# Wo block: the transpose of the rows normalised for the feed-forward, and the two copies behind it, one row tile later

## The reference

```python
# x is (1, 2048, 1024); LN(v) = (v - mean) / sqrt(var + 1e-5) over the last axis
q, k, v = LN(x) @ Wq, LN(x) @ Wk, LN(x) @ Wv           # 16 heads of 64, rotary on q and k
attn = softmax(causal(q k^T) / 8) v                     # per head, then the heads side by side
x = x + LN(attn @ Wo)
gate, up = LN(x) @ Wg^T, LN(x) @ Wu^T                   # Wg, Wu, Wd: 4-bit codes and block scales
x = x + LN((silu(gate) * up) @ Wd^T)
```

## Time and profile before

| | |
|---|---|
| time, median of 3 runs | 3079.66 us (3079.39 to 3079.66) |
| time of the profiled execution | 3079.91 us |
| span of the profiled execution | 3078.1 us |
| mean granted clock of TensorE | 0.960 of full speed |
| PE, PEld, DVE, ACT, POOL busy | 89%, 48%, 68%, 59%, 20% of the span |
| the Wo block in the span | its first transpose starts at 1311.3 us, its last copy ends at about 1558.0 us |

### The profile page before, as it was taken

The page is one execution under the profiler, slowest core; times in us unless marked ns, Lnnn a source line. Parts: engine busy times, 40 slices in busy tenths (PEclk is TensorE's granted clock), DMA queues, the critical chain, the costliest instruction groups (busy, mean ns, idle before and its releaser), DMA issues. The chain is left out here.

```text
span 3078.1 us, 55127 instructions
## 1 busy us (share of the span) xinstructions
PE 2738.7 (89%) x19792; PEld 1476.4 (48%) x19792; DVE 2106.7 (68%) x3522; ACT 1830.1 (59%) x2483; POOL 601.1 (20%) x399
## 2 busy tenths in 40 slices
PE   4998999789999999588808999999999999999996
PEld 2443444267777777444403444444444444444442
DVE  6544555577777777345567877877777777777867
ACT  2113434268888988712267677766767667676642
POOL 0000000067778878500120000000000000000002
PEclk9998999789999999899959999999999999999998
DMA  4312222322222221112221111111111111111124
GB/s 164 119 51 89 82 75 68 89 77 77 77 76 62 73 75 49 59 62 75 74 64 55 49 50 48 48 55 46 52 49 49 50 49 48 55 50 45 53 69 164
DMA packets 84361, 209.43 MB, mean 68 GB/s; under 512 B 13840, under 2 KB 14224, under 8 KB 83856
## 3 DMA queue, kind: packets, MB, share of 16 engines
q1 hardware_dynamic: 84112, 206.17, 21.5%
HBM read 172.49 MB, written 33.62 MB: 67 GB/s over the span
## 5 line engine op out<-in xcount | busy, mean ns | idle before, releaser
L1334 PE MATMUL gp<-region,wgu 128*128 128x512 f16 x4224 | 930.3, 383 | 90.0 <-DVE wgu L1492 90.0
L1371 ACT ACTIVATE line<-code,offsets 128x512 f32<-128x512 f32 x1056 | 697.1, 713 | 111.2 <-DVE below L1470 45.5
L1334 PEld LDWEIGHTS gp<-region,wgu 128*128 128x128 f16 x4224 | 415.7, 99 | 600.9 <-issue 109.9
L732 POOL TENSOR_TENSOR pt_pair<-probs,pt_pair 128x1024 f16<-128x1024 f32 (+1 forms) x256 | 524.2, 2072 | 167.0 <-ACT probs L900 162.7
L1347 PE MATMUL yp<-wd,inter 128*128 128x512 f16 x2112 | 464.8, 381 | 24.8 <-DVE wd L1492 17.7
L940 DVE TENSOR_REDUCE mx<-sx 128x1 f32<-128x512 f32 (+3 forms) x640 | 360.6, 604 | 144.4 <-PE sx L833 115.5
L305 POOL TENSOR_TENSOR st<-st,eps 128x1 f32<-128x1 f32 x64 | 22.3, 348 | 1883.0 <-DVE st L1018 1639.2
L895 ACT ACTIVATE pt_pair<-st,coef 128x1024 f16<-128x1024 f32 (+1 forms) x320 | 318.2, 994 | 70.3 <-PE st L814 55.8
L550 PE MATMUL pq<-region,wt_pair 128*128 128x512 f16 x1536 | 334.2, 381 | 15.3 <-DVE wt_pair L601 15.3
L1347 PEld LDWEIGHTS yp<-wd,inter 128*128 128x128 f16 x2112 | 206.2, 98 | 279.8 <-issue 25.5
L900 ACT ACTIVATE probs<-st,coef 128x1024 f32<-128x1024 f32 (+1 forms) x320 | 317.8, 993 | 6.9 <-POOL pt_pair L732 6.4
(11 more groups left out here) (116 smaller groups left out, 3442.2 us busy)
## 6 DMA issues: line engine op xcount, KB each, us to landing
qk_pairs<-r_pair SPq DMA_DIRECT2D x128, 128.0 KB, 2.1
k<-qk_pairs SPq DMA_DIRECT2D x48, 256.0 KB, 5.3
cst<-in_gate_codes SPq DMA_DIRECT2D x44, 256.0 KB, 2.7
sst<-in_gate_scales SPq DMA_DIRECT2D x88, 128.0 KB, 3.0
cst<-in_up_codes SPq DMA_DIRECT2D x44, 256.0 KB, 2.7
sst<-in_up_scales SPq DMA_DIRECT2D x88, 128.0 KB, 3.0
cst<-in_down_codes SPq DMA_DIRECT2D x44, 256.0 KB, 2.8
sst<-in_down_scales SPq DMA_DIRECT2D x88, 128.0 KB, 3.1
```

Of the source, the lines that this page charges most:

```text
L732: eng.tensor_tensor(pt_pair[:, n0(u, g) % PT_RING, 1, 0:w], probs[:, n0(u, g) % P_RING, 0:w], pt_pair[:, n0(u, g) % PT_RING, 0, 0:w], ALU. ...
L1334: mm = pe.matmul(gp[:, e % 2, m, :], wgu[:, par, m, a, col0:col0 + P], xnT[:, b, k, tok], start=(k == 0 and a == b), stop=(k == KT - 1 and ...
L1371: a.activation(line[:, k % 4, :], code7[:, :], ACT.Identity, scale=slope, bias=offsets[:, k:k + 1]).then_inc(s_L.sem, 1)
```

## The change

In the Wo block, T5 and the two copies behind it are moved by one step. In step i, PE now does T4(i+1), MM(i), T5(i-2); ACT copies `tp5` of tile i-3 in place of i-2; and DVE computes the low half of `xnT` of tile i-3 in place of i-2. The pipelines of ACT and DVE are one step longer at the end (`after` is 3), with which their hardware loop covers steps 4 to 13, where it covered 2 to 13. No buffer and no wait is added or taken away; POOL and SP are untouched. The whole diff:

```diff
@@ -1087,8 +1087,8 @@
                         mm.then_inc(s_mm.sem, 1)
-                    if st.has(-1, ST):
-                        i, u = st.item(-1), st.slot(-1)
+                    if st.has(-2, ST):
+                        i, u = st.item(-2), st.slot(-2)
                         pe.wait_ge(s_xn.sem, s_xn.done(i))
                         pe.wait_ge(s_xlo.sem, s_xlo.room(i))
                         for k in range(KT):
@@ -1106,8 +1106,8 @@
                 def step(st):
-                    if st.has(-2, ST):
-                        i = st.item(-2)
+                    if st.has(-3, ST):
+                        i = st.item(-3)
                         a.wait_ge(s_t5.sem, s_t5.done(i))
                         a.activation(xnT[:, 0, :, bass.ds(i * P, P)], tp5[:, :, :], ACT.Copy
                                      ).then_inc(s_xhi.sem, 1)
@@ -1122,7 +1122,7 @@
-                pipeline(a, step, 2, 2, ST)
+                pipeline(a, step, 2, 3, ST)
@@ -1165,7 +1165,7 @@
-                pipeline(v, step, 2, 2, ST)
+                pipeline(v, step, 2, 3, ST)
```

## The result

The changed kernel takes 3047.99 us (median of four runs, 3047.22 to 3048.81) against 3079.66 us before. The ratio is 0.9895, with a 95% interval from 0.9878 to 0.9913: faster by about 1.0%. The forecast was 3047.7 us. That the two agree to 0.3 us is in part luck, since the four runs themselves lie 1.6 us apart.

What follows compares the result with a forecast made beforehand. A loop through TensorE and VectorE set the 14.27 us round; after the change TensorE's 12.12 us would. Later start, shorter rounds and shorter end bring T5(15) 32.0 us earlier: median 3047.7 us, range 3045.0 to 3054.0.

Steps and rivals of the forecast that it cites:

- The loop: Wo block before the change: TensorE and VectorE each wait for the other once a round, 2.43 + 11.79 + 0.05 = 14.27 us.
- TensorE's round of 12.12 us: Wo block after the change: TensorE's own work sets the round, 10.36 matmuls + 0.88 T4 + 0.88 T5, at most 12.17 us.
- The start: First T5 of the Wo block: T5(0) follows MM(1), T4(3) and MM(2), starting at 1350.90 us, 9.57 us later than before.
- The end: Last tiles of the Wo block: T5(13) to T5(15) takes 14.16 us against 25.79, with one VectorE chain left there.
- 1.3 us of drain: End of the Wo block: tile 14's low half stands behind the last VectorE chain and delays T5(15), an extra 1.3 us.
- VectorE's margin: Wo block rounds: VectorE alone takes 11.84 us, 0.28 under TensorE's 12.12; rival that VectorE is the bound, chance 0.07.
- The sum: Whole kernel: T5(15) starts 32.0 us earlier, so a profiled execution takes 3047.9 us and the median is 3047.7 us.
- The clock: Wo block: clock at 1.00 outside its two ends; rival that dips persist, 3053 us, chance 0.06.
- my list of waits: Wo block, other waits keep slack: `at` ends 9.3 us behind a T5, where MM(i) starts 13.9 us behind it.

## Why the prediction was right, step by step

- **The loop.** Right, and shown from three sides: TensorE's work is not in it before the change (the kernel before with 44 matmuls), each half of the change alone leaves it closed and costs time, and with both both waits go.
- **TensorE's round of 12.12 us.** From T5(0) at 1351.51 to T5(12) at 1496.79 it is 145.28 / 12 = 12.11 us. That the transposes take 0.88 us once not stalled was right (1412.91 - 1412.04 = 0.87).
- **The start.** T5(0) was to come at 1350.90 and came at 1351.51. Of the 0.6 us, 0.14 is a later start of the block (its first transpose at 1311.41, before at 1311.27), and the rest is the first group of matmuls, which kept the lower clock a little longer (11.69 us for the 48, before 11.21).
- **The end.** T5(13) to T5(15) was to take 14.16 us and took 1522.09 - 1508.02 = 14.07. The 1.3 us of drain is there, and removing it showed no gain in the time of the whole.
- **VectorE's margin.** The one term that was mis-sized: 0.28 us a round in the prediction, 0.42 measured, from a round of 11.69 in place of 11.84. VectorE's wait before L1140 was nevertheless close to the stated 0.3 (4.0 us in twelve waits): it is counted from the end of `xn`, while without a wait L1140 would start 0.09 us before that end, and 0.42 - 0.09 = 0.33.
- **The sum.** T5(15) moved by 1553.75 - 1522.09 = 31.7 us (32.0 forecast), the profiled span by 31.1. From the last low half to the end of the span it is 1520.06 us before and 1520.65 after, a difference of 0.6 us that is within the 3.4 us by which this stretch varies between profiled executions; the medians differ by 31.67.
- **The clock.** That the stretches at the lower clock would go with the waits was right: 1.00 in the block. The rule of the Trainium skill, page "TensorE: Matmul & The Clock Gate", section "What's actually happening", that idleness brings the slow clock, agrees with all windows here: over the rounds, 1.00 in the changed kernel and with VectorE's added work (waits of 0.7 us), 0.97 before, 0.95 before with fewer matmuls, 0.94 with only the copies moved, 0.81 with only the transpose moved. The sustained rate of 131 ns that the Trainium skill names on the same page, section "Back-to-back issue gap", is not what the traces show: the groups keep 216 ns in every run at full clock.
- **What my list of waits lacked.** The prediction gave MM(i)'s wait for `at` of tile i-2 a slack of 4.6 us, and that was enough for the change itself. For the transpose moved alone I did not work it out again, and there it ended last and set the start of the matmuls, 3.6 us later than I had it. A slack belongs to an order, not to a buffer.

## What to carry to other kernels

When two engines each wait for the other once a round and neither is full, add up the loop (here 2.43 + 11.79 + 0.05 = the 14.27 us of the round) and move the whole hand-over, the producer's step and all its consumers' steps, by one tile; moving one side alone closes the loop over another buffer and can cost more than it had. Before such a move, work out each engine's own round: the larger one (12.11 against 11.69 here) is what the time falls to if no other wait is left, and only from then on does cutting that engine's work pay. One tile of distance is enough once no wait is left, and each further one costs its pass at the end.

## What the runs showed that I had not expected

- Taking work off TensorE while it waits in a loop gained nothing and seems to have cost a little: 44 matmuls in place of 48 a tile, in the kernel before, gave 3083.14 us against 3079.82 us for the runs beside it, with an interval of the ratio that begins at 1.0000. Its waits grew from 1.95 to 2.8 us, and some T5 that stand in the loop ran at the lower clock (1.97 us against 1.09).
- The price of a broken order is in the clock too: with only the transpose moved, the 48 matmuls of the round shown took 12.37 us in place of 10.52.
- On VectorE, a low half that has nothing to wait for started 0.08 to 0.09 us before the end of the instruction ahead of it; over a round that was worth 0.15 us against my sum.
